# Two passes over the blocks instead of two halves per block in an expert stage, and its loops written out

## The reference

```
h1 = jnp.einsum('bsd,edh->bseh', x, W1)
h2 = jnp.einsum('bsd,edh->bseh', x, W2)
expert_out = jnp.einsum('bseh,ehd->bsed', jax.nn.silu(h1) * h2, W3)
out = jnp.einsum('bsed,bse->bsd', expert_out, gate_prob)
```

## Time and profile before

| | |
|---|---|
| median of 3 runs | 977.32 us (975.43 to 977.99) |
| the profiled execution | 976.63 us, its span 974.6 us |
| PE / DVE / ACT / POOL busy | 79% / 60% / 50% / 25% of the span |
| mean granted clock of TensorE | 0.884 of full speed |
| layer-2 expert stage, first to last turn of a gated product | 426.44 to 538.35 us |
| layer-3 expert stage, the same | 711.20 to 951.09 us |

### The profile page before, as it was taken

How to read it: one execution, slowest core, us unless ns; L and a number is a source line. 1 busy time by engine, 2 the same in 40 slices (tenths; PEclk the granted TensorE clock), 3 DMA queues, 4 the chain that set the end, 5 groups by cost and what they waited for, 6 DMA issues and landing times. The chain is left out here.

```text
span 974.6 us, 18563 instructions
## 1 busy us (share of the span) xinstructions
PE 769.4 (79%) x6364; PEld 431.3 (44%) x6365; DVE 583.4 (60%) x1274; ACT 486.8 (50%) x619; POOL 241.2 (25%) x260
## 2 busy tenths in 40 slices
PE   3859558899897897489999396886599995599993
PEld 1857426533663555443333253554534442234341
DVE  3975443399767662666666466663676663366652
ACT  4134125543244554266776143443377774377771
POOL 1051000277020100135563111441132220122110
PEclk8579757999989999599999697899599998799996
DMA  3000055000034320601111334861504002530004
GB/s 115 1 0 1 0 180 219 1 0 1 1 102 141 81 55 5 230 26 39 43 38 33 121 99 135 261 190 34 203 24 152 22 18 79 204 145 22 22 11 135
DMA packets 52574, 77.69 MB, mean 80 GB/s; under 512 B 9668, under 2 KB 45636, under 8 KB 49316
## 3 DMA queue, kind: packets, MB, share of 16 engines
q1 hardware_dynamic: 48040, 67.42, 21.1%
q0 software_dynamic: 4480, 9.58, 3.1%
HBM read 54.29 MB, written 9.96 MB: 66 GB/s over the span
## 5 line engine op out<-in xcount | busy, mean ns | idle before, releaser
L2257 PE MATMUL psum<-ring,f_x_t 128*32 x432 | 198.3, 602 | 1.5 <-DVE f_x_t L1976 1.5
L2262 PE MATMUL psum<-f_w_up,f_x_t 128*32 128x512 f32 x864 | 198.7, 602 | 0.0
L1991 DVE COPY f_w_up<-ring 128x2048 f32 x108 | 130.7, 1226 | 94.1 <-issue 66.8
L2126 ACT ACTIVATE f_w_down<-ring 128x1024 f32 x108 | 107.7, 1047 | 0.0
L2281 PE MATMUL psum<-ring,f_gated_t 128*32 x432 | 102.1, 379 | 1.7 <-issue 1.7
L2285 PE MATMUL psum<-f_w_down,f_gated_t 128*32 128x256 f32 x1296 | 102.8, 379 | 0.0
L2262 PE MATMUL psum<-x,f_x_t 128*32 128x512 f32 x216 | 99.6, 605 | 0.0
L2262 PE MATMUL psum<-h,f_x_t 128*32 128x512 f32 x216 | 98.7, 600 | 0.0
L2257 PEld LDWEIGHTS psum<-ring,f_x_t 128*32 128x32 f32 x432 | 43.5, 111 | 110.3 <-issue 110.3
L2117 ACT ACTIVATE x<-ring 128x2048 f32 x27 | 51.7, 1915 | 52.5 <-issue 41.3
L2281 PEld LDWEIGHTS psum<-ring,f_gated_t 128*32 128x32 f32 x432 | 47.4, 110 | 61.1 <-issue 33.3
(11 more groups left out here) (304 smaller groups left out, 1633.3 us busy)
## 6 DMA issues: line engine op xcount, KB each, us to landing
ring<-in_f_experts SPq DMA_DIRECT2D x24, 1536.0 KB, 7.4
a_stack_q<-a_parts SPq DMA_DIRECT2D x96, 64.0 KB, 2.0
a_stack_k<-a_parts SPq DMA_DIRECT2D x96, 64.0 KB, 2.0
rows_in<-h SPq DMA_DIRECT2D x4, 1024.0 KB, 12.5
ring<-rows_out SPq DMA_DIRECT2D x8, 512.0 KB, 5.7
ring<-in_a_wqkv SPq DMA_DIRECT2D x2, 768.0 KB, 4.0
x_in<-in_x SPq DMA_DIRECT2D x1, 1024.0 KB, 5.7
out<-x SPq DMA_DIRECT2D x4, 256.0 KB, 2.1
```

What stands on the lines that cost most here:

```text
L1991: dve.tensor_copy(w_up[tile, b], k.ring[:, bass.ds(at[tile - 1] + CHUNK_COLS * c, 2 * CT * CHUNK)]).then_inc(s_uv, 1)
L2126: act.activation(w_down[:, tile - 1, b, :], k.ring[:, bass.ds(at[tile - 2] + (CHUNK_COLS * c + 2 * CT * CHUNK), CHUNK // P * C)], ACT.Copy ...
L2257: pe.matmul(psum[0:QUARTER, 2 * b + side, :], x_t[:, xb, t, 0:QUARTER], k.ring[:, bass.ds(at + (CHUNK_COLS * c + start), CHUNK)], start=fi ...
L2262: last = pe.matmul(psum[rows, 2 * b + side, :], x_t[:, xb, t, rows], w_up[tile, b][:, start:start + CHUNK], start=first, stop=final, tile_ ...
```

## The change

Layer 3 goes over all 18 blocks twice. Pass 1 uses the first half of each expert's inner units, pass 2 the second. `chunks` becomes `passes`, and there are `STEPS = passes * MAXBLK` steps: 18 in layer 2, 36 in layer 3, as before. The ring holds one chunk of each of the 8 experts. In pass 1 y is stored plainly to a new DRAM tensor `earlier_y`; in pass 2 POOL loads it back and `take_y` adds it to the PSUM bank, and only then is it scattered to `rows_out`. x is gathered and turned in each step. SP loads the second half of expert e when pass 1 is through with expert e.

All steps of both layers are written out instead of loops, with fixed indices, so POOL's index copies go. Layer 3 takes over the opening that layer 2 has. The ring columns of a coming step are read by DVE before `take_y` and by ACT before `take_gated`. The table needs no step that wraps an expert's number around the ring. In pass 2 `wait_loaded` reads the load count and waits before each `copy_up` of DVE (quarter 1) and ACT.

```diff
@@ load_chunk, experts_ffn
-    place = CHUNK_COLS * (n % RING_CHUNKS)
-    column = CHUNK_COLS * (n % chunks)
-    sp.dma_start(k.ring[:, place:place + CHUNK_COLS], weights[n // chunks, :, column:column + CHUNK_COLS]).then_inc(loaded[n % chunks], 16)
+    place, column = CHUNK_COLS * e, CHUNK_COLS * part
+    sp.dma_start(k.ring[:, place:place + CHUNK_COLS], weights[e, :, column:column + CHUNK_COLS]).then_inc(loaded[part], 16)
...
+        def wait_loaded(eng, step):
+
+            if step >= MAXBLK:
+                loads = eng.value_load(table[0:1, 1, step % MAXBLK, 3:4], min_val=16, max_val=16 * E)
+                eng.wait_ge(s_loaded[1], loads)
+                eng.wait_ge(s_table, 1)
@@ sync
-            sp.wait_ge(s_table, 1)
-            for e in range(RING_EXPERTS, E):
-                done = sp.value_load(free_at[0:1, e - RING_EXPERTS:e - RING_EXPERTS + 1], min_val=1, max_val=4 * MAXBLK)
-                for c in range(chunks):
-                    sp.wait_ge(s_loaded[c], 16 * e)
-                    sp.wait_ge(s_dn[c], done)
-                    load_chunk(sp, k, w["experts"], chunks, chunks * e + c, s_loaded)
+            if passes == 2:
+                sp.wait_ge(s_table, 1)
+                sp.wait_ge(s_loaded[0], 16 * E)
+                for e in range(E):
+                    if e:
+                        sp.wait_ge(s_loaded[1], 16 * e)
+                    if e < E - 1:
+                        done = sp.value_load(free_at[0:1, e:e + 1], min_val=1, max_val=4 * MAXBLK)
+                        sp.wait_ge(s_dn, done)
+                    else:
+                        sp.wait_ge(s_dn, 4 * MAXBLK)
+                    load_chunk(sp, k, w["experts"], e, 1, s_loaded)
@@ gpsimd (new)
+            def load_x(step):
+                j, b = step % MAXBLK, step % 2
+                if step >= 2:
+                    pool.wait_ge(s_xt, step - 1)
+                pool.indirect_dma_start(out=xs[:, b, :], out_offset=None, in_=k.rows_in,
+                                        in_offset=bass.IndirectOffsetOnAxis(ap=from_row[:, j:j + 1], axis=0)).then_inc(s_x[b], 16)
+
+            def store_y(step):
+                j, b = step % MAXBLK, step % 2
+                pool.wait_ge(s_y, step + 1)
+                if step < STEPS - MAXBLK:
+                    pool.dma_start(k.earlier_y[P * j:P * j + P], y[:, b, :]).then_inc(s_yd[b], 16)
+                else:
+                    pool.indirect_dma_start(out=k.rows_out, out_offset=bass.IndirectOffsetOnAxis(ap=to_row[:, j:j + 1], axis=0),
+                                            in_=y[:, b, :], in_offset=None).then_inc(s_yd[b], 16)
+
+            def load_earlier_y(step):
+                j, b = step - MAXBLK, step % 2
+                pool.wait_ge(s_yd[b], 16 * (j // 2 + 1))
+                pool.wait_ge(s_y, step - 1)
+                pool.dma_start(earlier_y[:, b, :], k.earlier_y[P * j:P * j + P]).then_inc(s_ey[b], 16)
+
+            load_x(0)
+            load_x(1)
+            for step in range(STEPS):
+                if step + 2 < STEPS:
+                    load_x(step + 2)
+                if step == 2:
+                    pool.wait_ge(s_to, 1)
+                if step >= 2:
+                    store_y(step - 2)
+                if step >= MAXBLK:
+                    load_earlier_y(step)
+            store_y(STEPS - 2)
+            store_y(STEPS - 1)
@@ vector (new)
+            def take_y(q):
+
+                b = q % 2
+                dve.wait_ge(s_dn, 4 * (q + 1))
+                if q >= 2:
+                    dve.wait_ge(s_yd[b], 16 * (q // 2))
+                if q < MAXBLK:
+                    dve.tensor_copy(y[:, b, :], psum[:, Y_BANK, 0:C]).then_inc(s_y, 1)
+                else:
+                    dve.wait_ge(s_ey[b], 16 * ((q - MAXBLK) // 2 + 1))
+                    dve.tensor_tensor(y[:, b, :], earlier_y[:, b, :], psum[:, Y_BANK, 0:C], ALU.add).then_inc(s_y, 1)
...
+            for q in range(STEPS):
+                if q + 1 < STEPS:
+                    copy_up(q + 1, ahead, 1)
+                    take_x(q + 1)
+                    copy_up(q + 1, ahead, 2)
+                copy_down(q, at)
+                gate(q)
+                at = ahead
+                if q + 2 < STEPS:
+                    ahead = ring_columns(mybir.EngineType.DVE, q + 2, pair)
+                if q:
+                    take_y(q - 1)
+            take_y(STEPS - 1)
@@ scalar (new)
+            for q in range(STEPS):
+                if q + 1 < STEPS:
+                    ahead = ring_columns(mybir.EngineType.Activation, q + 1, pair)
+                if q:
+                    take_gated(q - 1)
+                if q + 1 < STEPS:
+                    copy_up(q + 1, ahead)
+                silu_of(q)
+                copy_down(q, at)
+                at = ahead
@@ tensor (new)
+            turn_x(0)
+            up(0, at)
+            turn_x(1)
+            for q in range(1, STEPS):
+                ahead = ring_column(q)
+                turn_gated(q - 1)
+                if q + 1 < STEPS:
+                    turn_x(q + 1)
+                up(q, ahead)
+                down(q - 1, at)
+                at = ahead
+            turn_gated(STEPS - 1)
+            down(STEPS - 1, at)
```

More of the change, by code:

```diff
@@ L1655, with load_chunk, experts_ffn @@
 ATTENTION_CHUNKS = 6
-PAIRED = (MAXBLK + 1) // 2 * 2
 QUARTERS = TOK // QUARTER
-def above_zero(count):
-    return not isinstance(count, int) or count > 0
-def load_chunk(sp, k, weights, chunks, n, loaded):
-    place = CHUNK_COLS * (n % RING_CHUNKS)
-    column = CHUNK_COLS * (n % chunks)
-    sp.dma_start(k.ring[:, place:place + CHUNK_COLS], weights[n // chunks, :, column:column + CHUNK_COLS]).then_inc(loaded[n % chunks], 16)
-def experts_ffn(nc, sem, sbuf, psum, k, w, chunks, s_loaded, tag, finish=None):
-    RING_EXPERTS = RING_CHUNKS // chunks
+def load_chunk(sp, k, weights, e, part, loaded):
+    place, column = CHUNK_COLS * e, CHUNK_COLS * part
+    sp.dma_start(k.ring[:, place:place + CHUNK_COLS], weights[e, :, column:column + CHUNK_COLS]).then_inc(loaded[part], 16)
+def experts_ffn(nc, sem, sbuf, psum, k, w, passes, s_loaded, tag, finish=None):
+    STEPS = passes * MAXBLK
+    assert RING_CHUNKS == E and MAXBLK % 2 == 0
     with ExitStack() as ctx:
@@ L1792, in experts_ffn, with ring_columns @@
         block = ctx.enter_context(nc.Block())
-        PAIRS = MAXBLK // 2 - 1
-        assert MAXBLK % 2 == 0
+        def ring_columns(engine, step, tiles):
+            _, columns = nc.values_load_multi_w_load_instructions(
+                table[0:1, 0, step % MAXBLK, tiles], [engine], min_val=0, max_val=(E - 1) * CHUNK_COLS)
+            return columns
+        def wait_loaded(eng, step):
[3 more added lines that the diff above has]
+                eng.wait_ge(s_table, 1)
         @block.sync
@@ L1801, in _ @@
                 sp.dma_start(dst[:], src).then_inc(s_w, 16)
-            for n in range(ATTENTION_CHUNKS, RING_CHUNKS):
-                load_chunk(sp, k, w["experts"], chunks, n, s_loaded)
+            for e in range(ATTENTION_CHUNKS, E):
+                load_chunk(sp, k, w["experts"], e, 0, s_loaded)
             sp.wait_ge(ln.s_out, TT)
@@ L1849, in store_y @@
[L1849 to L1859, removed]
@@ L2062, in turn, with take_x @@
[L2062 to L2070 removed]
+            def take_x(q):
+                dve.wait_ge(s_xt, q + 1)
+                dve.tensor_copy(x_t[:, q % 2].rearrange("p t n -> p (t n)"), psum[:, X_BANK, 0:C]).then_inc(s_xto, 1)
@@ new lines, in _ @@
+            dve.wait_ge(s_table, 1)
+            dve.wait_ge(s_loaded[0], 16 * E)
+            pair = slice(1, 3)
+            at = ring_columns(mybir.EngineType.DVE, 0, pair)
+            ahead = ring_columns(mybir.EngineType.DVE, 1, pair)
+            copy_up(0, at, 1)
+            copy_up(0, at, 2)
+            take_x(0)
+            for q in range(STEPS):
[10 more added lines that the diff above has]
+                    take_y(q - 1)
@@ L2256, in up @@
                         first, final = t == 0, t == CT - 1
[L2257 to L2259 removed]
+                        pe.matmul(psum[0:QUARTER, 2 * b + side, :], x_t[:, b, t, 0:QUARTER],
+                                  k.ring[:, bass.ds(at + start, CHUNK)], start=first, stop=final, tile_position=(0, 0))
                         for tile in range(1, 4):
                             rows = slice(QUARTER * tile, QUARTER * tile + QUARTER)
[L2262 removed]
+                            last = pe.matmul(psum[rows, 2 * b + side, :], x_t[:, b, t, rows],
                                              w_up[tile, b][:, start:start + CHUNK], start=first, stop=final,
```

368 lines of the change are left out of this document (88 added, 280 removed).

## The result

The changed kernel took 942.9 us (median of 4, 938.09 to 943.38), beside 977.15 for the kernel before: ratio 0.964 with an interval of 0.961 to 0.967. A second series gave 941.95 us, ratio 0.9638 (0.9621 to 0.9655). 942 was forecast.

The account below looks back on a forecast made before the run. TensorE, 79% busy, was taken as the bound, with ring waits holding up layer 3. Layer 2's 9.6 us plus layer 3's 25.4 made 35.0 off 976.63, 941.6, plus 0.7 for the median: 942 us, range 935 to 958.

Parts of the forecast that it names:

- Layer 2 written out: Layer 2's 18 steps without loops: all run at 6.11 us, first to last turn 111.9 to 103.6, gain 8.3 us.
- PE's floor: TensorE's own time per step without idle: 6.11 us with an x block turned, about 5.88 without.
- the reads' new place: Register reads moved ahead of y, into idle time; without this cover each 0.1 us costs 5.4 us.
- Layer 3: Two passes over a ring of eight remove both long waits: first to last turn 239.9 to 213.6, gain 26.3 us.
- Pass 2's additions at nothing: Pass 2's load-count read (0.73 us) and y addition on DVE and ACT cost 0, at most 5 us.
- Each tenth of a microsecond costs 54 x 0.1: Over the steps of both layers, register reads not hidden behind the down copies would cost 5.4 us per 0.1 us.
- POOL: Pass 2's gather, scatter and reload take 5 us of each 6.11 us step, hidden; reload 1.3 us within 0.5 to 2.6.
- rival of 8.6 us a step: POOL binds pass 2, all three DMAs taking 2.55 us: 45 us more, 987 us; chance 4%.
- The ends: Table preparation, openings and last scatters: layer 2 gains 0.6 and 0.7 us; layer 3 loses 1.6 and gains 0.7.
- the pace of 6.45: Rival: register reads in each step make all steps of both layers run at 6.45 us: 960 us; chance 12%.
- PE never waited for gathered rows: Rival: x gathers land late under ring loads, 0.9 us behind PE for seven loads: 6 us, 948 us; chance 10%.
- DVE waited for the ring's loads: Rival: the ring still holds pass 2 up, one or two 10 us waits return: 952 to 962 us; chance 4%.

Follow-up runs that it names:

- the written-out kernel: The kernel before with only its four expert-stage loops written out as straight code; ring of four, index copies and read places kept: 964.79 us, ratio 0.9862.
- the experiment with six: The changed kernel with six more 32 KB loads of a constant issued by POOL behind each reload in pass 2: 966.63 us, ratio 0.9902.

## Why the prediction was right

The profiled execution went from 976.63 to 938.09 us. Split by the stages the sum had named (rows of DVE's `from_row`, where the opening starts; before, then after):

```profile
410.02 0.18 DVE L1939 TENSOR_SCALAR f_from_row<-psum 128x18 uint32<-128x18 f32 x1 [0.47 <-PE psum L2235]
...
697.08 0.18 DVE L1939 TENSOR_SCALAR f_from_row<-psum 128x18 uint32<-128x18 f32 x1 [0.48 <-PE psum L2235]
```
```profile
405.80 0.18 DVE L1942 TENSOR_SCALAR f_from_row<-psum 128x18 uint32<-128x18 f32 x1 [0.48 <-PE psum L2138]
...
685.09 0.18 DVE L1942 TENSOR_SCALAR f_from_row<-psum 128x18 uint32<-128x18 f32 x1 [0.48 <-PE psum L2138]
```

| gain, us | predicted | measured |
|---|---|---|
| layer 2, first to last turn | 8.3 | 111.91 - 105.16 = 6.75 |
| layer 2, opening to first turn | 0.6 | 16.42 - 16.07 = 0.35 |
| layer 2, last turn to last scatter's end | 0.7 | 5.91 - 5.16 = 0.75 |
| layer 3, first to last turn | 26.3 | 239.89 - 213.36 = 26.53 |
| layer 3, opening | -1.6 | 14.12 - 15.74 = -1.62 |
| layer 3, end | 0.7 | 5.90 - 5.17 = 0.73 |
| sum | 35.0 | 33.5 |

The medians differ by 34.3 and 35.5 us in the two series. The profiled pair differs by 5 us more than the sum; 4.2 of these are there before layer 2's opening begins (410.02 against 405.80), in stages whose work the change leaves alone, so they are not counted as its gain.

1. *Layer 2 written out:* the pace came out at PE's floor. But by the written-out kernel the loops are only 5.8 us of this gain; by the rows of its trace the other 2.6 are the second pair of ring columns that DVE read in one gap in every second step. The prediction gave the whole to the loops, under the cover of the reads' new place, which turned out not to be needed for the pace. 1.65 us of the 8.3 were lost to the slow first step, which I had not thought of. I had borrowed layer 2's opening for layer 3 and priced its idle time at 2.4 us, but not what idle time does to PE's clock.
2. *Layer 3:* the ring was the cause, as the chain had said: writing out the loops leaves both waits (27.8 us), two passes remove them. In the written-out kernel the two long steps and the slow one behind them take 16.54 + 18.30 + 7.68 us, 24.5 more than three normal ones; less 3.9 for the x blocks turned again that is 20.6, and the changed kernel is 234.09 - 213.36 = 20.7 us shorter from first to last. The floor held over all 35 intervals.
3. *Pass 2's additions at nothing:* right, with the load-count read at 0.39 us, not 0.73, and the addition no dearer than the copy. DVE still waited 0.25 us for PE's product before its gate; taking out the whole hand-over changed nothing. "Each tenth of a microsecond costs 54 x 0.1" was never called on: even both reads behind y left all but two steps at the pace.
4. *POOL:* 1.46 + 1.46 + 1.03 with one gap of 0.30 is 4.3 us of 6.10, for the 5 I took. The reload's 1.46 is inside 0.5 to 2.6. Its rival of 8.6 us a step was far off; with six more DMAs the bound moves to POOL, as 84.94 of 92 us busy show (the experiment with six), so the mechanism is real, and it doesn't show at 4.9 us of work a step. The section "Who interferes with whom" of the Trainium skill's "SBUF — State Buffer" has GpSimd's writing of descriptors wait for fast DVE copies. The traces allow it but don't show it: the reload takes 1.46 us where DVE copies of 1.22 and 0.69 us lie over it, and 0.56 at least; with six loads behind it the same reload took 0.69 on average, and no run here takes DVE's copies away.
5. *The ends:* right within 0.3 us each.
6. *The chances:* the forecast and the four rivals already add up to 100%, so the 1% for what I don't see and the 2% for no change had no room.

Of the rivals, the pace of 6.45 appeared nowhere in the changed kernel (its like, 6.42, is in the written-out one, where DVE reads two blocks' columns in one gap); from 690 to 925 us PE never waited for gathered rows, though gathers took up to 8.0 us to land; and DVE waited for the ring's loads for 0.8 us at most.

## What to carry to other kernels

When a buffer's turn-over stalls the pace, change the order of the work so that a slot's next content is wanted a whole pass later; the price here was 0.22 us of PE for each block turned again, and the partial results through DRAM cost nothing, with the engine that issues their DMAs at work for 4.3 us of each 6.1, and still for 4.9. When a loop is written out, look for what its body did twice: here the written-out loop kept a register read that a plain order of steps doesn't need. Copies that run a step ahead want their data a step ahead too: count lateness from the copy, not from the matmul. Price idle time of PE at the opening of a stage with the slow step that can follow it (1.4 to 3 us here), and keep everything that PE delivers late, such as the next block's x, behind the first gate.

## What was not expected of the hardware

- The clock fell after idle time of 2.85 us in 13 of 17 openings, while PE was already busy again (0.69 of full speed in 421 to 425 us), and three times so long that the step took over 9 us. Why the old order's layer 2, with the same 2.85 us idle, never showed it stays open.
- A plain DMA issued by POOL took between 0.56 and 1.48 us for the same 128 KB (median 1.46 for the reload), and 0.60 on average for a 64 KB one. With six more loads a step the reload took 0.69 on average, but the added ones 0.71, though they were only 32 KB. What sets these durations stays open.
- The read of the load count cost 0.39 us of DVE between two of its instructions in pass 2 (0.74 once, in its first step), about half of the 0.73 that a difference of two gaps had given. A pair of ring columns cost 0.77 us in the written-out kernel, two pairs in one gap 1.91.
